# DVE's order in the second attention's loop: the copy of a slot's turned piece ahead of the maxima of the slot two on

## The reference

```python
q = apply_rope(x @ Wq)        # 32 heads of 16 columns
k = apply_rope(x @ Wk)        # 8 key/value heads of 16 columns
v = x @ Wv
scores = einsum('bhqd,bhkd->bhqk', q, repeat(k, 4)) / sqrt(16)
scores = where(key > query, lowest, scores)     # causal, 512 x 512 a head
attn = softmax(scores)
ctx = einsum('bhqk,bhkd->bhqd', attn, repeat(v, 4))
x = layernorm(x + ctx @ Wo)
```

## Time and profile before

| | |
|---|---|
| median of 3 runs | 1178.65 us (1178.55 to 1179.78) |
| the profiled execution | 1180.05 us, its span 1178.4 us |
| PE busy | 1138.7 us (97%) |
| DVE busy | 778.3 us (66%) |
| ACT busy | 705.6 us (60%) |
| POOL busy | 410.9 us (35%) |

### The profile page before, as it was taken

How to read it: one execution, slowest core, us unless ns; L and a number is a source line. 1 busy time by engine, 2 the same in 40 slices (tenths; PEclk the granted TensorE clock), 3 DMA queues, 4 the chain that set the end, 5 groups by cost and what they waited for, 6 DMA issues and landing times. The chain is left out here.

```text
span 1178.4 us, 20479 instructions
## 1 busy us (share of the span) xinstructions
PE 1138.7 (97%) x6634; PEld 954.3 (81%) x6634; DVE 778.3 (66%) x2463; ACT 705.6 (60%) x1646; POOL 410.9 (35%) x342
## 2 busy tenths in 40 slices
PE   7899999999999999999999999999999899999997
PEld 6788888888888888888888778888888677777786
DVE  6767776667776677766677762222336799999775
ACT  6666665566665566666566544543113799999524
POOL 4554554355444455534443513434013210010200
PEclk9999999999999999999999999999999999999999
DMA  6011110101110110100100012222001223321001
GB/s 230 19 36 37 40 33 28 31 28 36 47 36 20 38 31 24 55 27 11 45 19 28 1 37 80 62 80 73 1 18 28 50 71 78 100 52 34 2 1 72
DMA packets 30364, 51.24 MB, mean 43 GB/s; under 512 B 5680, under 2 KB 6576, under 8 KB 30256
## 3 DMA queue, kind: packets, MB, share of 16 engines
q1 hardware_dynamic: 29680, 48.85, 14.4%
q10 hardware_dynamic: 576, 1.05, 0.2%
HBM read 38.35 MB, written 2.10 MB: 34 GB/s over the span
## 5 line engine op out<-in xcount | busy, mean ns | idle before, releaser
L487 POOL TENSOR_TENSOR turned<-turned,sin 128x512 f32<-128x512 f32 x73 | 94.5, 1294 | 311.6 <-ACT turned L347 311.6
L363 ACT ACTIVATE probs<-probs,neg_max 128x256 f32<-128x256 f32 (+1 forms) x256 | 119.8, 473 | 14.0 <-DVE neg_max L580 14.0
L1477 ACT ACTIVATE a_probs<-a_probs,a_neg_max 128x512 f32<-128x512 f32 (+3 forms) x256 | 122.6, 563 | 0.1
L1661 DVE CUSTOM_DVE_ANT_0 a_probs<-bank,a_mask 128x512 f32<-128x512 f32 (+3 forms) x256 | 109.8, 486 | 7.8 <-PE bank L1881 7.8
L490 POOL TENSOR_TENSOR turned<-turned,by_cos 128x512 f32<-128x512 f32 x73 | 101.2, 1386 | 5.7
L96 PE MATMUL bank<-wo_hi,oT_hi 128*128 128x512 f32 x256 | 100.3, 392 | 1.6 <-DVE oT_lo L643 1.6
L734 PE MATMUL bank<-xT_hi,wq_hi 128*128 128x512 f32 x256 | 101.7, 397 | 0.0
L734 PE MATMUL bank<-xT_lo,wq_hi 128*128 128x512 f32 x256 | 100.3, 392 | 0.0
L734 PE MATMUL bank<-xT_hi,wq_lo 128*128 128x512 f32 x256 | 100.1, 391 | 0.0
L96 PE MATMUL bank<-wo_hi,oT_lo 128*128 128x512 f32 x256 | 99.9, 390 | 0.0
L96 PE MATMUL bank<-wo_lo,oT_hi 128*128 128x512 f32 x256 | 99.7, 389 | 0.0
(11 more groups left out here) (234 smaller groups left out, 3158.8 us busy)
## 6 DMA issues: line engine op xcount, KB each, us to landing
staged<-weights SPq DMA_DIRECT2D x70, 256.0 KB, 2.7
f_staged<-weights_f SPq DMA_DIRECT2D x33, 256.0 KB, 2.7
a_q_stack<-a_qT_hi SPq DMA_DIRECT2D x64, 64.0 KB, 2.0
rows<-x_rows SPq DMA_DIRECT2D x2, 1024.0 KB, 7.4
a_k_stack<-a_kT_hi SPq DMA_DIRECT2D x64, 32.0 KB, 2.0
a_q_stack<-a_qT_lo SPq DMA_DIRECT2D x32, 64.0 KB, 2.0
out<-rows SPq DMA_DIRECT2D x8, 256.0 KB, 2.0
a_raw<-weights_qkv SPq DMA_DIRECT2D x4, 384.0 KB, 4.4
```

The source lines that it names most:

```text
L363: act.activation(probs[:, s % 2, h, 0:width], probs[:, s % 2, h, 0:width], ACT.Exp, bias=neg_max[:, s % 2, h:h + 1], scale=SCALE0, accum_o ...
L487: pool.tensor_tensor(at, at, sin[:, :], ALU.mult).then_inc(sin_done, 1)
L1477: act.activation(row_probs(s, qt), row_probs(s, qt), ACT.Exp, bias=neg_max[:, h, qt:qt + 1], scale=-1.0).then_inc(exp_done, 1)
L1661: dve.tensor_tensor_reduce(row_probs(s, qt), ps_s[bank][:, at:at + seen], mask[:, SEQ - seen:SEQ], -SCALE1, HIGHEST, ALU.add, ALU.min, neg ...
```

## The change

In DVE's list, `copy_turned(s)` moves from behind `maxima(s + 2)` to ahead of it. At s mod 4 = 2 it thus comes right behind `evacuate`. Nothing else changes: instructions, operands, semaphores and the lists of the other engines are the same.

```diff
             for s in range(SLOTS1 + 3):
                 if s % GROUP1 == 2 and s >= GROUP1:
                     evacuate(s // GROUP1 - 1)
+                if s < SLOTS1:
+                    copy_turned(s)
                 if s + AHEAD_MAXIMA < SLOTS1:
                     maxima(s + AHEAD_MAXIMA)
-                if s < SLOTS1:
-                    copy_turned(s)
                 if s in PARTS_IN_LOOP:
                     low_part(PARTS_IN_LOOP[s])
                 if s % GROUP1 == 3 and GROUP1 <= s < SLOTS1:
                     join(s // GROUP1 - 1)
```

## The result

The change makes the kernel slower: 1214.13 us (median of 4 runs, 1213.45 to 1215.79) against 1178.62, a ratio of 1.0301 (95% interval 1.0288 to 1.0313). Forecast were 1208 and a range of 1202 to 1221. The profiled execution took 1213.96, its span 1212.3, 33.9 more than the span before.

What follows compares the result with a forecast made beforehand. It took PE, ACT and DVE, all nearly full, to bound the loop. Beginning +1.8, middle +27.6 and end -0.9 gave 28.4, with 1.0 for the clock +29.4 on 1180.05; on the median 1208, range 1202 to 1221.

Steps and rivals of the forecast that it cites:

- The mechanism: In the loop, the copy's wait heads DVE's queue and closes two overlapping lines into one; a unit 13.0 us, not 11.03.
- 1.0 for the clock: Early slots, near 930 us: a fall to the 1.2 GHz level expected, taken as +1.0 us.
- the ring: In each slot, copy, maxima, third piece of scores and next turn wait for one another in a circle; 3.25 us.
- the last: From the last maxima readout's end, through the third piece of scores, to the next turn's first transpose; 0.24 us.
- The first link: From the first transpose of a turn on PE to the start of DVE's copy; 0.69 us.
- the second: DVE's copy, from its start to the start of the maxima behind it; 0.60 us.
- The ring's own bounds: In the loop, 3.16 to 3.34 us a slot, -5 to +5; with the early clock 0 to +2, 1202 to 1214.
- The cover by the engines' other work: In the loop, PE's product part (by 0.08 us), DVE's `evacuate` and `join`, and ACT's work stay hidden beside the ring.
- the rival of repeated falls: The clock falls again in each of 14 steady units, adding 8 to 22 us: 1217 to 1230; chance 0.13.
- Early release wins: In the loop, a copy done before PE asks removes PE's wait, 4.8 us less: 1174; chance 0.03.
- order costs nothing: In the loop, DVE's total work sets the pace, so nothing changes: 1179 or a few us more; chance 0.03.
- a shorter ring: In the loop, PE runs part of the next turn ahead or links overlap: 3.05 a slot, 1197; chance 0.04.

Runs made afterwards that it cites:

- e1: The changed kernel with one extra DVE instruction of about 0.2 us ahead of the copy in slots 4 to 61; 1214.26 us.
- e5: The changed kernel with the copy behind the first two of the four maxima instead of ahead of all; 1182.7 us.
- e6: The changed kernel with the copy behind three of the four maxima instead of ahead of all; 1182.7 us.
- e8: The changed order only in the two slots of each unit with the product, from slot 4 on, the others as in the kernel before; 1188.6 us.
- e10: The changed order from slot 4 on, the first four slots as in the kernel before, one more wait instruction included; 1212.93 us.
- e7: The changed order only in the two slots of each unit without the product, from slot 4 on, the others as in the kernel before; 1206.55 us.
- e11: The kernel before with PE's last three turned parts (slots 0 to 2) ahead of the scores instead of behind; 1175.54 us, ratio to the kernel before 0.9975.

## Why the prediction was right, and by what it was short

The mechanism held in each of its steps. (The turns, maxima and scores that the prediction numbers 6, 8 and 9 at 960 us, and 8 and 11 at 965 and 967, are those of slots 14, 16 and 17, and 16 and 19; they have the same place in their unit, and no sum hangs on it.) By marks of the two profiles:

| stretch | forecast | measured |
|---|---|---|
| to the start of maxima(8) | +1.8, and 1.0 for the clock | 941.00 - 938.11 = +2.9 |
| maxima(8) to maxima(63) | +27.6 | 1124.23 - 941.00 - 151.2 = +32.0 |
| maxima(63) to the last copy | -0.95 | 3.80 - 4.83 = -1.0 |
| sum | +29.4 | +33.9 |

*The term that was mis-sized is the ring's length*, 3.25 taken and 3.32 measured, 55 times: 3.9 us of the 4.5 missing. Of its four links the last was the worst: 0.28, not 0.24. My only row for it had 0.28, with other transposes; I shortened it by a case in which PE had not waited. In the changed kernel PE waits there in every slot. The first link was 0.71 for 0.69, the second 0.61 for 0.60. The other 0.7 us is two slots of 3.67 each, up to the copies of slots 32 and 53. The excess lies in the first link, 1.06 instead of 0.71, behind a turn that took its usual time:

```profile
1025.98 1.26 PE L1899 MATMUL bank<-identity,a_probs 128*128 128x128 f32 x10
...
1027.04 0.69 DVE L1669 COPY f_pT<-bank 128x512 f32<-128x512 f32 x1 [0.71 <-PE bank L1899]
```

The kernel before has irregular slots at the same numbers, e1 has none. What holds DVE up there is open.

*The range* was right with some luck. The ring's own bounds gave 1202 to 1214, and 1214.13 lies at their upper edge; the part up to 1221 was for a rival that failed.

*The cover by the engines' other work* was right, with little to spare (0.08 by the forecast, 0.16 of wait in the weight load by the profile): the slots with the product have the beat of those without, `join` and `evacuate` fall into DVE's wait, and e1 shows that a further 0.2 us goes in for nothing.

*The clock.* I had expected one fall in the first slots and priced it at 1.0; there were two, at 917.6 and 927.9, granted 0.51 and 0.50. That this stretch came out as forecast is in part luck: DVE began 0.29 earlier than I had put (915.69 for 915.98), and from there it took 15.49 us to maxima(5) (at 931.18) instead of 14.15, so that the two falls cost about 1.3 together, an estimate from these marks. In the loop the rival of repeated falls failed: the clock was granted in full from 931.3 to the end of the loop, with PE busy for 11.73 of 13.28 us (I had put 10.7 of 13.0, so PE idles less than I said).

```profile
955.02 0.49 PE L1881 MATMUL bank<-a_k_stack,a_q_stack 96*128 96x512 f32 x1 [0.80 <-DVE a_neg_max L1661]
...
971.00:1110.00 139.00, 122.59 (x961) 85.03 (x960) 109.69 (x409) 116.73 (x252) 6.33 (x12) 1.00 0.24 59
```

As the prediction read the Trainium skill, "TensorE: Matmul & The Clock Gate", section "A second HAM failure mode: psum-queue depth-cycling", the clock would have swung. That section tells of another kernel and gives no size for the gaps; gaps of up to 0.8 us ahead of the scores did not do it here.

*Early release wins; order costs nothing; a shorter ring:* all three fell, the first by e5 and e6 as well, where the ring is out of the way, the last by the 3.32.

*The rest.* The medians are 35.5 apart, the two spans 33.9. The profiled execution of before lies 1.4 above its median, that of after 0.2 below its own, so 1.6 of the 6.1 us between forecast and result is in which execution was profiled. No run was made to see whether the stretch at half clock set the former apart, but the times on record point that way. The kernel before ran 17 times beside e5 to e8: nine times in 1177.80 to 1178.38, with a mean granted clock of 0.997 or 0.998, and eight times in 1179.57 to 1179.99, six of these with 0.995 or 0.996, as the profiled one (0.996).

## What to carry to other kernels

Before an instruction with a wait is moved to the head of an in-order list, follow what stands behind it there: who waits for that, what is queued behind this one on its engine, and whether the move's own wait is at the end. If it is, add up one turn of the ring and compare it with the loop's beat, here 3.32 against 11.03 / 4 = 2.76. Work on the ring costs its full length in every turn, work in the gaps of it costs nothing, and it can be opened at any engine, not only where it was closed. Where PE waits for a piece of a product, take the link behind it from a case in which PE waits as well.

## What the runs showed that was not expected

- The fall of the clock near 930 us is not a property of the kernel's early slots. e10 and e8 have the same copies as the kernel before up to slot 3 (3.94, then 3.87 to 3.89 apart) and show the full clock there; e7, with the same slots, shows 0.50. The orders part only in slot 4, about where the clock fell, but up to the fall PE's rows agree in all four profiles, in their lengths and in their waits (0.87 and 0.18 to 0.20 us ahead of the scores, 0.31 ahead of turn(4)). And the kernel before, run again unchanged, has the two groups of times above. e10 and e7:

```profile
926.80:934.00 7.20, 5.84 (x46) 3.89 (x45) 5.26 (x19) 6.93 (x16) 3.33 (x6) 1.00 0.05 11
```

```profile
931.00:934.40 3.40, 3.40 (x21) 1.29 (x20) 1.14 (x5) 2.85 (x7) 1.30 (x3) 0.50 0.00 0
```

- A gain that has nothing to do with the change was lying in the same loop: three sets of four transposes, ahead of the scores instead of behind, are worth 2.9 us (e11).
- With the changed order from slot 4 on (e10) nearly every slot takes 3.35, not 3.32, and none 3.67. The 0.03 is in the first link, from the turn's start at 1000.97 to the copy at 1001.71, 0.74 instead of 0.71:

```profile
1000.97 1.26 PE L1902 MATMUL bank<-identity,a_probs 128*128 128x128 f32 x10
...
1001.71 0.69 DVE L1669 COPY f_pT<-bank 128x512 f32<-128x512 f32 x1 [1.02 <-PE bank L1902]
```

Ahead of the copy e10 has the one more wait instruction that its edit left there, and e7's slots in the changed order have it too and take 3.35 as well. That this wait is the cause fits both, but it was not tested by itself.
